# The experts' down projection as three float32r products of high and low parts

## What is computed

```
xn  = layernorm(x)                              # x: 4 x 2048 x 256
out = x + attention(xn) + experts(xn)
```

```
topk_idx, topk_w = routing of each token to 8 of 64 experts (4 of 8 groups)
buf = the tokens of each expert, in order, at most CAP = 256        # 64 x 256 x 256
g = einsum('ech,ehi->eci', buf, w_gate)                             # i = 128
u = einsum('ech,ehi->eci', buf, w_up)
y = einsum('eci,eih->ech', silu(g) * u, w_down)                     # the down projection
out = the sum of y, times topk_w, over the experts of each token
```

## Time and profile before

| | |
|---|---|
| median of three executions | 1477.26 us |
| range of the three | 1475.11 to 1482.85 us |
| the profiled execution, its own time | 1481.57 us |
| its span in the trace | 1479.9 us |
| TensorE busy | 1333.5 us, 90% of the span |
| TensorE weight loads busy | 1152.0 us, 78% |
| VectorE busy | 1037.8 us, 70% |
| ScalarE busy | 461.9 us, 31% |
| GpSimd busy | 539.9 us, 36% |
| mean granted clock of TensorE | 0.97 |

### The profile page before, as it was taken

The page is one execution under the profiler, slowest core; times in us unless marked ns, Lnnn a source line. Parts: engine busy times, 40 slices in busy tenths (PEclk is TensorE's granted clock), DMA queues, the critical chain, the costliest instruction groups (busy, mean ns, idle before and its releaser), DMA issues.

```text
span 1479.9 us, 27132 instructions
## 1 busy us (share of the span) xinstructions
PE 1333.5 (90%) x9460; PEld 1152.0 (78%) x9460; DVE 1037.8 (70%) x2417; ACT 461.9 (31%) x791; POOL 539.9 (36%) x411
## 2 busy tenths in 40 slices
PE   2999798897989899889999999999999999999992
PEld 1778686776878787668888888888888888888872
DVE  4897878978789666876757667576675757756450
ACT  3433333323333232122333333333333333333320
POOL 3010000100001004753645636465463645636522
PEclk9999999998998999999999999999999999999996
DMA  5355333433343121125646646466464655646666
GB/s 192 131 200 198 119 119 118 150 105 103 118 137 124 59 83 43 73 58 156 153 116 162 163 125 160 105 171 148 130 162 112 165 140 141 155 136 150 189 204 225
DMA packets 134511, 203.47 MB, mean 137 GB/s; under 512 B 12400, under 2 KB 106160, under 8 KB 134320
## 3 DMA queue, kind: packets, MB, share of 16 engines
q1 hardware_dynamic: 108208, 161.10, 33.8%
q0 software_dynamic: 26240, 41.63, 14.7%
HBM read 153.33 MB, written 57.74 MB: 143 GB/s over the span
## 4 chain that ended last, share of the span: by engine, by line
PE 58%; DVE 23%; issue 7%; DMA 7%; SPq 2%; ACT 1%; POOL 1%; DVEq 1%; POOLq 0%; ACTq 0%
PE bank L676 15%; PE bank L795 6%; PE bank L771 6%; PE bank L688 5%; PE bank L751 5%; PE bank L736 4%; PE bank L718 4%; PE bank L804 3%; PE bank L739 3%; DVE Dt L1229 3%; DMA arena<-in_L_ffn_w_down_dram 3%; PE bank L700 2%; DMA out_dram<-arena 2%; PE bank L709 2%; PE bank L785 2%
## 5 line engine op out<-in xcount | busy, mean ns | idle before, releaser
L544 POOL DMA_INDIRECT arena<-table,idx_all x132 | 167.9, 1272 | 270.2 <-DVE arena L1332 224.3
L552 POOL DMA_INDIRECT acc<-arena,idx_all x128 | 226.3, 1768 | 80.3 <-DMA acc<-arena,idx_all 45.8
L676 PE MATMUL bank<-xp,wq 128*128 128x512 f32 x768 | 212.0, 412 | 0.0
L676 PE MATMUL bank<-xp,wk 128*128 128x512 f32 x768 | 208.5, 407 | 0.0
L676 PEld LDWEIGHTS bank<-xp,wk 128*128 128x128 f32 x768 | 142.4, 192 | 31.3 <-issue 0.2
L1229 DVE TENSOR_TENSOR_SCAN Dt<-decay,eye_b 128x512 f32<-128x512 f32 x128 | 159.9, 1251 | 2.5 <-DMA decay<-decay_dram 2.5
L676 PEld LDWEIGHTS bank<-xp,wq 128*128 128x128 f32 x768 | 139.2, 193 | 25.9
L517 POOL DMA_DIRECT2D table<-arena x16 | 12.4, 777 | 371.2 <-DVE arena L1157 371.2
L718 PE MATMUL bank<-qT,kT 128*128 128x128 f32 x1024 | 139.4, 280 | 2.7 <-ACT kT L942 2.7
L942 ACT ACTIVATE qT<-bank 128x512 f32<-128x512 f32 x128 | 76.5, 598 | 198.2 <-PE bank L676 153.0
L751 PEld LDWEIGHTS bank<-V,kw 128*128 128x128 f32 x960 | 122.1, 195 | 20.4 <-issue 10.8
(11 more groups left out here) (156 smaller groups left out, 2268.5 us busy)
## 6 DMA issues: line engine op xcount, KB each, us to landing
decay<-decay_dram SPq DMA_DIRECT2D x64, 512.0 KB, 5.7
carry<-decay_dram SPq DMA_DIRECT2D x60, 512.0 KB, 4.5
arena<-in_L_attn_x_dram SPq DMA_DIRECT2D x16, 512.0 KB, 4.6
table<-arena SPq DMA_DIRECT2D x16, 512.0 KB, 2.9
xT_dram<-arena SPq DMA_DIRECT2D x16, 512.0 KB, 3.0
xs<-xT_dram SPq DMA_DIRECT2D x16, 512.0 KB, 5.4
arena<-in_L_ffn_w_gate_dram SPq DMA_DIRECT2D x64, 128.0 KB, 2.6
arena<-in_L_ffn_w_up_dram SPq DMA_DIRECT2D x64, 128.0 KB, 3.0
```

What stands on the lines that cost most here:

```text
L544: pool.indirect_dma_start(out=xg[:, e % 2, j, :], out_offset=None, in_=table[:, :], in_offset=bass.IndirectOffsetOnAxis(ap=idx_all[:, e, j ...
L552: pool.indirect_dma_start(out=acc[:, :], out_offset=bass.IndirectOffsetOnAxis(ap=idx_all[:, e, j:j + 1], axis=0), in_=yb[:, e % 2, j, :], ...
L676: last = mm(bank[which][:, :], w[:, part, k, h * DK:(h + 1) * DK], xp[:, other, k, :], start=(k + i == 0), stop=(k == KD - 1 and i == 2))
```

## The change

The loaded down weights and the hidden values get a high and a low part each, and the down projection becomes three float32r products for each half of the tokens. ScalarE makes the high parts (`down_high_e`, `hidden_high`), VectorE the low ones (`down_low_e`, `hidden_low`). The new weights' parts have a tile of their own, `wd_p`; the hidden values' parts go where the token parts `xgT` were. `expert_down` waits for both low parts. In ScalarE's list `down_high_e` stands at place 0 behind `expert_tokens`, `hidden_high` at place 1 between `expert_gate` and `weights_high_e`. In VectorE's list `down_low_e` and `hidden_low` stand at place 2 between `expert_hidden` and `weights_low_e`.

```diff
+        wd_p = sb("wd_p", [P, 2, D], F32R)
+        h_p = xgT[:, :, 0:CAP]
...
+        wd_high, wd_split, h_full, h_high = sem("wd_high"), sem("wd_split"), sem("h_full"), sem("h_high")
...
             def expert_down(c, j):
                 e = (c - E0) * STEP_E + j
                 pe.wait_ge(h_ready, e + 1)
+                pe.wait_ge(wd_split, e + 1)
                 for half in range(NHALF):
-                    last = mm(bank[7][:, half * D:(half + 1) * D], hT[:, half * P:(half + 1) * P],
-                              wde[:, j % 2, :], start=True, stop=True)
+                    for i, (part, other) in enumerate(PARTS):
+                        last = mm(bank[7][:, half * D:(half + 1) * D], h_p[:, part, half * P:(half + 1) * P],
+                                  wd_p[:, other, :], start=(i == 0), stop=(i == 2))
                 last.then_inc(y_ps, 1)
...
+            def down_high_e(c, j):
+                act.wait_ge(ew_in[j % 2], ((c - E0) * (STEP_E // 2) + j // 2 + 1) * 48)
+                f(wd_p[:, 0], wde[:, j % 2], ACT.Copy).then_inc(wd_high, 1)
+
+            def hidden_high(c, j):
+                act.wait_ge(h_full, (c - E0) * STEP_E + j + 1)
+                f(h_p[:, 0], hT, ACT.Copy).then_inc(h_high, 1)
...
-                if kind == "experts" and place == 1 and 0 < s < H:
-                    weights_high_e(c, s)
+                if kind == "experts" and s > 0 and place == 0:
+                    down_high_e(c, s - 1)
+                if kind == "experts" and place == 1 and s > 0:
+                    hidden_high(c, s - 1)
+                    if s < H:
+                        weights_high_e(c, s)
...
-                tt(hT, hT, bank[7][:, CAP:2 * CAP], ALU.mult).then_inc(h_ready, 1)
+                tt(hT, hT, bank[7][:, CAP:2 * CAP], ALU.mult).then_inc(h_full, 1)
+
+            def hidden_low(c, j):
+                dve.wait_ge(h_high, (c - E0) * STEP_E + j + 1)
+                tt(h_p[:, 1], hT, h_p[:, 0], ALU.subtract).then_inc(h_ready, 1)
+
+            def down_low_e(c, j):
+                dve.wait_ge(wd_high, (c - E0) * STEP_E + j + 1)
+                tt(wd_p[:, 1], wde[:, j % 2], wd_p[:, 0], ALU.subtract).then_inc(wd_split, 1)
...
                         expert_hidden(c, s - 1)
+                        down_low_e(c, s - 1)
+                        hidden_low(c, s - 1)
                         if s < H:
                             weights_low_e(c, s)
```

## The result

The changed kernel takes 1508.65 us (median of six runs, 1505.87 to 1509.87) against 1478.89 for the kernel before (six runs): a ratio of 1.020, interval 1.0174 to 1.0221. It is 29.8 us slower; forecast was 34 slower, at 1511.

A forecast was written before the change was run, and what follows sets the result against it. TensorE's next transposes were taken as held by VectorE's scaling, with almost no slack. Per step 0.79 + 1.01 - 0.82 + 1.01 + 0.79 + 1.01 + 0.45 + 0 = 4.24 us, eight steps 34: 1477.26 + 34 = 1511; range 1490 to 1528.

The forecast's parts named there:

- The bound: Expert steps: TensorE 97% busy, yet its next transposes (L785) start 0.14 us after VectorE's scaling (L1332), almost no slack.
- rival 1: Down projection: TensorE's gain survives, 0.21 us for each of 64 experts, 13.4 us faster, to 1464; chance 6%.
- The new waits: ScalarE-VectorE hand-offs after the sigmoid: hidden copy at 1.33 us, its subtraction at 1.79, next weights' low part at 2.32.
- Slots 1 and 5: Odd expert slots of each step: next transposes (L785) at 5.08 us after the sigmoid, 0.79 later than 4.29.
- Slot 3: Expert slot whose weights arrive late: that wait goes, transposes fall from mean 5.90 to 5.08 us, 0.82 less.
- Slot 7: Expert slot with a smaller late-weights delay: transposes go from mean 4.63 to 5.08 us, 0.45 more.
- Slot 8: Last slot of a step: next chunk's split ends at 3.35 us, TensorE follows at 3.49 against 3.46; adds nothing.
- Slots 2, 4 and 6: Even expert slots: scaling starts at 4.99 us in place of 3.97, transposes at 6.00, 1.01 later.
- TensorE's 0.21 us: Down projection: six float32r matmuls take 0.71 us in place of 0.92, 0.21 less per expert, lost in the wait.
- rival 2: Expert slots: only engine time counts as hand-offs overlap, +12.6 us, to 1490; L1320 would start before 2.0; chance 12%.
- Rival 3: Expert slots: hand-offs cost more, +60 us, to 1537, with TensorE waiting at L688 for the next chunk's split; chance 9%.
- A sign that failed: TensorE's busy share in the expert stage should fall to about 91 to 92%.

The follow-up runs named there:

- early loads: Kernel before with the scaling on ScalarE and gate and up loads issued once their split is done: 1456.28 us, ratio 0.9861.
- The products alone: Kernel before with six float32r matmuls on high parts only, both low parts left out, nothing added to VectorE's queue: 1476.6 us, ratio 0.999.

## Why the prediction was right

The direction, the place and the mechanism held, and 29.8 us slower stand against 34. Step by step:

- *The bound.* Right: the share of 97% was no protection, and TensorE now waits for the scaling in every slot from 1 to 7. But the 0.14 us between scaling and transposes, which rival 1 counts as slack, is the hand-off itself: where TensorE stands waiting it starts 0.14 to 0.15 us behind the scaling's end too (702.83 to 702.97 in the earlier trace rows, 783.51 to 783.66 above). In the kernel before there was no slack to speak of: with the scaling out of VectorE's queue and early loads its transposes start at 4.28 and 4.98, against 4.29 and 4.99, so the scaling arrived just when TensorE's own order came to the transposes. The products alone do not show this bound. With nothing added to VectorE's queue the shorter product came through, 0.12 to 0.16 us in each of six slots; late weights in the other two gave nearly half of it back.
- *The new waits.* Right to 0.02 us: hidden copy 1.33 (forecast 1.33), low part 1.78 (1.79), next weights' low part 2.30 (2.32). The trace's ScalarE copy of 128x256 from SBUF takes 0.42 us, the value taken from rows. The estimate by the Trainium skill (ScalarE: Activation LUTs, section What ACT_TABLE_LOAD costs) was 0.40. The cover named for the weights' subtraction was shown by moving that line (no change) and the price of a line behind the wait by adding one (+0.15 a slot).
- *Slots 1 and 5*: 0.77 more (forecast 0.79). *Slot 3*: 5.09 on the average in place of 5.90, 0.81 less (0.82); the weights' wait is gone. *Slot 7*: 5.06 (5.08). *Slot 8*: the next chunk's split ends at 3.34 and TensorE follows at 3.49, as forecast; the way from the slot's sigmoid to the next step's is 24.50, 0.09 less than before (0).
- *Slots 2, 4 and 6*: 0.86 more, forecast 1.01. This is the term that was mis-sized. "L1272 to L1332 is 2.06" was taken as VectorE's own pace; it is 1.92 now (780.72 to 782.64). In the slot of the earlier trace rows the scaling (803.09) started 0.15 us after the plain down projection's end and 0.73 after the state's update in front of it; now, with the projection long done, it follows the same update (L1305) by 0.60. So 0.14 us of the 2.06 were a wait for the projection. The products alone agree: with a shorter projection and VectorE's queue otherwise as before, the transposes of even slots came 0.14 us sooner (4.85). Three slots, eight steps, 0.15: 3.6 us of the 4.2 that the forecast was too high. The two lines of the kernel before:

```profile
801.86 1.08 PE L804 MATMUL bank<-arena 128*128 128x256 f32 x4
...
802.36 0.69 DVE L1288 TENSOR_TENSOR state<-state,bank 128x512 f32<-128x512 f32 x1
```

- *TensorE's 0.21 us* was too much as well: 0.76 in place of 0.71 in the chain, so 0.16 saved. It did not reach the sum, since the wait took it, but rival 1's price would have been 10 and not 13 us.
- *The rivals.* Rival 1 and rival 2 fall by the slots: L1345 starts at 2.30, not before 2.0, and L788 waits for L1357 in all 53 slots. Rival 3's wait at L688 (now L691) came to hundredths at most: the split of slot 8 in the second step ends at 841.47 and L691 starts at 841.62, but the way to the next step is shorter than before, not longer.
- *A sign that failed.* TensorE's busy share came to 94%, not to 91 or 92. Over seven whole steps, before and then after, its busy time has not fallen at all (620.1 and 621.7 us), though each projection advances it by less; the steps have only grown longer:

```profile
677.66:1314.54 636.88, 620.09 (x4481) 546.84 (x4480) 422.63 (x707) 209.78 (x372) 341.54 (x224) 1.00 0.58 144
...
673.18:1336.02 662.84, 621.72 (x4593) 549.39 (x4592) 463.53 (x819) 246.65 (x483) 333.47 (x224) 1.00 0.57 139
```

## What to carry to other kernels

A split that goes from one engine to another and back puts a round trip at the head of an in-order queue, and everything behind it pays: put work that is ready in front of the wait, on both engines. Before crediting a shorter operation of the busiest engine, follow the ring that lets it start its next piece (here down projection, scaling on VectorE, next transposes, all in one bank): it was already level with TensorE's own order at a busy share of 97%, so all that was added to it had to be paid. And a gap between two lines is only a pace if nothing in it waits: look at what the second line could have been waiting for before using the gap as a price.

## What the runs showed that was not expected

Six float32r matmuls of 128x256 that stand alone advance TensorE by 0.76 us, 0.127 each, where twelve of the gate and up products take 1.42, 0.118 each. And a faster TensorE brings its own late weights: with the products alone, slot 3 grew from 5.90 to 6.15 us by the time at which its loads land, and together with slot 7 it gave back 0.40 of the 0.86 us a step that the other slots had won.
